# Rotated keys of the fifth layer: one full-width sum on VectorE and a head-table multiplication on GpSimd

## The reference, cut to what matters

```python
def _L2_xattn_ref(x, mem_seq, mem_mask, rms_scale, q_w, kv_w, out_w):
    ...
    q = jnp.einsum('BTD,NDH->BTNH', xn, q_w)
    kv = jnp.einsum('BSD,cKDH->cBSKH', mn, kv_w)
    k, v = (kv[0], kv[1])
    ...
    q = _apply_rope(q, q_pos) * HEAD_DIM ** (-0.5)
    k = _apply_rope(k, k_pos)
    q = q.reshape(B, T, NUM_KV, G, HEAD_DIM)
    logits = jnp.einsum('BTKGH,BSKH->BKGTS', q, k, preferred_element_type=jnp.float32)
    masked = jnp.where(mem_mask[:, None, None, None, :], logits, MASK_FILL)
    probs = jax.nn.softmax(masked, axis=-1).astype(x.dtype)
```

## Time and profile before

| | |
|---|---|
| median of 3 executions | 4558.1 us (4556.83 to 4559.51) |
| profiled execution, its own time | 4552.95 us |
| its span, first to last instruction | 4551.1 us |
| mean granted TensorE clock | 0.866 of 2.4 GHz |
| busy over the span | PE 87%, PEld 68%, DVE 66%, ACT 38%, POOL 17% |
| fifth layer | from 2901.1 us (the layer's first memset) to 3285.4 us (its last residual) |

### The profile page before, as it was taken

One profiled execution on the slowest core, in us unless ns is written; L12 is line 12 of the kernel. 1 busy time (PEld: TensorE's weight loads), 2 busy tenths in 40 slices (PEclk: granted clock), 3 DMA queues, 4 the chain that ended last, 5 costly groups with the idle time before them and its releaser, 6 DMA issues.

```text
span 4551.1 us, 105680 instructions
## 1 busy us (share of the span) xinstructions
PE 3947.3 (87%) x36890; PEld 3104.3 (68%) x36890; DVE 3006.2 (66%) x9082; ACT 1735.9 (38%) x4156; POOL 764.9 (17%) x575
## 2 busy tenths in 40 slices
PE   6999978888886888889999999777737899999965
PEld 4888855555554555589999999655537777777754
DVE  4666657777775777766666666799861355555569
ACT  3555534444442344333333333222203344444421
POOL 1222221111110000011111111100171122222211
PEclk9999987777776677689999999888758999999975
DMA  3000010000001000000000000100015200000000
GB/s 124 8 7 8 7 23 6 6 6 6 6 7 65 16 16 15 15 6 0 0 0 0 0 0 3 44 12 12 6 39 191 98 12 12 9 12 12 10 13 26
DMA packets 102053, 97.04 MB, mean 21 GB/s; under 512 B 31664, under 2 KB 91056, under 8 KB 101296
## 3 DMA queue, kind: packets, MB, share of 16 engines
q1 hardware_dynamic: 97408, 76.94, 5.6%
q0 software_dynamic: 4096, 8.40, 0.6%
q10 hardware_dynamic: 432, 10.19, 0.6%
HBM read 46.97 MB, written 19.66 MB: 15 GB/s over the span
## 4 chain that ended last, share of the span: by engine, by line
PE 60%; DVE 18%; SPq 8%; issue 7%; POOL 2%; DMA 2%; ACT 1%; DVEq 1%; POOLq 0%; ACTq 0%
PE ps L768 54%; SPq L591 7%; PE ps L936 5%; DVE acc L1658 2%; DMA arena_a<-kT 1%; DVE o_sb L1637 1%; POOL scr L718 1%; PE ps L806 1%; DVE arena_b L1606 1%; POOL route L740 1%; DVE xn L1442 1%; DVE x_sb L1557 1%; DVE st L1401 1%; DVE mx L1527 1%; DVE vsmall L1614 1%
## 5 line engine op out<-in xcount | busy, mean ns | idle before, releaser
L768 PE MATMUL ps<-xcT,small 128*128 128x256 f32 x2176 | 610.1, 419 | 34.7 <-DMA xcT<-in_ctxT 25.4
L732 POOL TENSOR_TENSOR rstd<-veps,neghalf 128x2 f32<-128x2 f32 (+1 forms) x224 | 167.9, 749 | 2403.8 <-DVE veps L1434 2071.2
L768 PEld LDWEIGHTS ps<-xcT,small 128*128 128x128 f32 x2176 | 411.3, 204 | 233.3 <-issue 114.5
L768 PE MATMUL ps<-arena_b,qT 64*64 64x64 f32 (+3 forms) x11136 | 541.8, 242 | 21.6 <-DVE arena_b L1606 20.3
L1278 ACT ACTIVATE kT<-ps 128x256 f32<-128x256 f32 (+1 forms) x768 | 294.4, 383 | 623.6 <-PE ps L768 547.4
L768 PE MATMUL ps<-small,xcT 128*64 128x64 f32 (+5 forms) x3072 | 482.7, 384 | 51.4 <-DVE acc L1658 30.3
L768 PE MATMUL ps<-xhi,parts_a 128*128 128x256 f32 (+1 forms) x2112 | 500.4, 289 | 22.7 <-DVE qT L1687 22.7
L768 PEld LDWEIGHTS ps<-arena_b,qT 64*64 64x64 f32 (+3 forms) x11136 | 463.5, 149 | 58.4 <-issue 35.0
L1248 ACT ACTIVATE pT<-ps 128x512 f32<-128x512 f32 (+1 forms) x576 | 303.3, 571 | 467.0 <-PE ps L936 465.3
L1687 DVE TENSOR_TENSOR qT<-kT,ps 128x256 f32<-128x256 f32 (+1 forms) x768 | 316.8, 419 | 188.5 <-ACT kT L1278 181.0
L768 PE MATMUL ps<-xlo,parts_a 128*128 128x256 f32 (+1 forms) x1536 | 430.6, 280 | 0.0
(11 more groups left out here) (212 smaller groups left out, 6388.5 us busy)
## 6 DMA issues: line engine op xcount, KB each, us to landing
wbuf<-parts_b SPq DMA_DIRECT2D x39, 512.0 KB, 3.0
arena_a<-kT SPq DMA_DIRECT2D x1024, 8.0 KB
xcT<-in_ctxT SPq DMA_DIRECT2D x96, 128.0 KB, 2.1
xn<-scr SPq DMA_DIRECT2D x39, 128.0 KB, 2.2
scr_y<-acc SPq DMA_DIRECT2D x39, 128.0 KB, 2.9
scr<-vsmall SPq DMA_DIRECT2D x9, 512.0 KB, 13.3
ctx_sb<-in_ctx SPq DMA_DIRECT2D x32, 128.0 KB, 2.1
arena_a<-in_w ACTq DMA_DIRECT2D x1, 4096.0 KB, 12.4
```

Source lines behind the costliest of these rows:

```text
L732: pool.tensor_tensor(rstd[:, 0:n], veps[:, 0:n], neghalf[:, 0:n], ALU.pow).then_inc(s_rstd.sem, 1)
L768: return nc.tensor.matmul(o, lhsT, rhs, start=start, stop=stop, skip_group_check=True)
```

## The change

DVE's four additions become one over 128 partitions and 256 columns, into the tile `kT` (unused in this layer until now). POOL then writes all four head blocks, zeros included, with one multiplication of 128 partitions x 1024 elements: the sum, read once for each head, times `own_rope`, a table of 128 x 4 that is 1 where the partition belongs to the head and 0 elsewhere. PE's `S0` now also waits for POOL (`s_krope`). POOL's memset of `k_rope` at the layer's start goes away. The table is made once, at the program's start, by a sum over blocks of 32 of the identity matrix on DVE.

```diff
@@ pool, start of L2X @@
+                    pool.wait_ge(s_krope0, 1)
                     for b in L1F.body_banks:
                         pool.wait_ge(drained[b], bank_base[4][b])
-                    pool.memset(arena_b[:, 0:2048], 0.0).then_inc(s_zero, 1)
                     pool.memset(vsmall[:, :, :], 0.0).then_inc(s_zero, 1)
@@ pool, do @@
+                if item == ("K", 0) and layer is L2X:
+
+                    u = layer.use(item)
+                    pool.wait_ge(drained[layer.front_ring.bank(g, u)], layer.front_ring.count(g, u))
+                    pool.tensor_tensor(k_rope(g.par).rearrange("p b (h k) -> p b h k", k=S),
+                                       k_sum(g.par).rearrange("p (b k) -> p b k", k=S).unsqueeze(2)
+                                       .to_broadcast([P, BPG, 4, S]),
+                                       own_rope[:, :].unsqueeze(1).unsqueeze(3).to_broadcast([P, BPG, 4, S]),
+                                       ALU.mult).then_inc(s_krope.sem, 1)
@@ pe, S0 @@
+                        if layer is L2X:
+                            pe.wait_ge(s_krope.sem, s_krope.after(g, 0))
@@ dve, start @@
-                    dve.wait_ge(s_zero, 4)
+                    dve.wait_ge(s_zero, 3)
...
+                    dve.tensor_reduce(own_rope[:, :], ident.rearrange("p (h d) -> p h d", d=32), AX_X,
+                                      ALU.add).then_inc(s_krope0, 1)
@@ dve, K of L2X @@
-                        for h in range(4):
-                            r0 = 32 * h
-                            last = dve.tensor_tensor(k_rope(g.par)[r0:r0 + 32, :, h * S:(h + 1) * S],
-                                                     c1[r0:r0 + 32], c2[r0:r0 + 32], ALU.add)
-                        last.then_inc(drained[b], 1)
+                        dve.wait_ge(s_krope.sem, s_krope.after(g.back(2), 0))
+                        dve.tensor_tensor(k_sum(g.par), qT[:, g.par, n + 2, :], qT[:, g.par, n + 3, :],
+                                          ALU.add).then_inc(drained[b], 1)
```

More of the change, by code:

```diff
@@ L289, in build @@
         onemu = sb("onemu", [P, 2])
+        own_rope = sb("own_rope", [P, 4])
         bv_col = sb("bv_col", [P, 1])
@@ L349, in build @@
         s_rope = step("s_rope", l2x=4)
+        s_krope = step("s_krope", l2x=1)
         s_mx = step("s_mx", **att)
@@ L383, in build @@
         s_bv = ctx.enter_context(nc.semaphore("s_bv"))
+        s_krope0 = ctx.enter_context(nc.semaphore("s_krope0"))
         s_ones = ctx.enter_context(nc.semaphore("s_ones"))
@@ L402, in build @@
         s_ready = ctx.enter_context(nc.semaphore("s_ready"))
-        steps = [s_stats, s_aggr, s_veps, s_rstd, s_xn, s_rope, s_mx, s_masked, s_sub,
+        steps = [s_krope, s_stats, s_aggr, s_veps, s_rstd, s_xn, s_rope, s_mx, s_masked, s_sub,
                  s_exp, s_sum, s_rv, s_probs, s_route, s_rexp, s_acc, s_act, s_mix, s_relu, s_upd, s_rank, s_xlo, s_res]
@@ L426, in k_rope, with k_sum @@
             return arena_b[:, par * 1024:(par + 1) * 1024].rearrange("p (b n) -> p b n", b=BPG)
+        def k_sum(par):
+            return kT[:, par, :]
         def v_small(par):
```

## The result

| | before | after |
|---|---|---|
| median of 5 executions | 4558.1 us (4555.49 to 4559.51) | 4581.23 us (4579.09 to 4584.71) |
| profiled execution, own time / span | 4552.95 / 4551.1 us | 4579.98 / 4577.4 us |
| mean granted TensorE clock | 0.866 | 0.863 |

The ratio is 1.0053, 95% interval 1.0038 to 1.0067: 23 us slower, 0.5%. Forecast were 4586 us, within 4571 to 4606.

A forecast was written before the change was run, and what follows sets the result against it. DVE, busy 94% of the layer's steady stretch, was taken to set the pace; +0.92 us a turn over 32 turns (29.4 us) less 1.5 at the starts gave +28 on 4558.1: 4586 us, range 4571 to 4606.

The forecast's parts named there:

- The sum: DVE's single remaining key addition of 128 x 256 from SBUF, in each turn: 0.42 us.
- DVE to POOL: Hand-over from DVE's last write of the key sum to POOL's start: 0.17 us.
- POOL's own time: POOL's multiplication of 128 x 1024 float32 in each turn: 1.90 us, with up to 2.2 allowed.
- The rival by which only the writes count: POOL's multiplication bound by its 1024 writes alone, 0.94 us, making the kernel faster: 4545 us; chance 4%.
- POOL made to wait for the running normalisation: POOL must let DVE's already started first normalisation finish before multiplying: 0.20 us.
- POOL to PE: Hand-over from POOL's multiplication to PE's start on the scores: 0.10 us.
- the half-clock seam: Stretch from key sum to softmax with scores at half clock, through PE: 4.21 us, against 3.17 before.
- The hold: DVE's normalisations from SBUF are held until POOL's multiplication ends; with POOL in second place, chance 57%.
- the case without one: Rival: normalisations not held and POOL not delayed, +0.59 us a turn, 4576 us; chance 19%.
- the full-clock seams: Stretches from key sum to softmax with scores at full clock, set by DVE's held work: 3.89 us.
- The wait added ahead of the sum: DVE's new wait, before the key sum, for POOL's work of two groups ago: costs nothing.
- The turn: One pipeline turn per group of 256 tokens in the fifth layer: from 11.7 to 12.6 us, +0.92.

The follow-up runs named there:

- first experiment: Changed kernel, but the fifth layer's four normalisations read unused PSUM banks instead of x and the context: 4582.09 us, ratio 1.0058.
- DVE's version of the multiplication: Changed kernel, but DVE adds the keys once and multiplies the four head blocks itself, POOL does nothing: 4562.99 us, ratio 1.0009.
- the run with M ahead of K: Changed kernel with the normalisations (M) ahead of the keys' sum (K) and the statistics ahead of the first softmax: 4596.7 us, ratio 1.0082.

## Why the prediction was right

The sign and the mechanism hold, and the time is near: 4581 against 4586 us. Part of that nearness is luck. The fifth layer was forecast to grow by 28 us and grew by 19.5; the fourth, in which nothing was forecast, grew by 3.9. By its steps:

- **The sum** 0.42, as measured. The table at the program's start costs 0.2 us, and DVE's work in the layer starts 1.7 us earlier, as forecast.
- **DVE to POOL** was taken as 0.17 and is 0.08 to 0.09. **POOL's own time** was taken as 1.90 from the other layers' multiplication: 1.89 with nothing beside it, so that spreading the second operand too costs nothing. The rival by which only the writes count falls.
- **POOL made to wait for the running normalisation**: taken as 0.20 from the earlier trace rows, it is 0.035 (1.927 against 1.892). That, 0.08 from the line above and 0.05 from **POOL to PE** (0.05 for 0.10) are the 0.3 us by which the half-clock seam was forecast too long: 4.21, measured 3.84 to 3.91.
- **The hold** is real, against the case without one, which had 19%. The Trainium skill (SBUF — State Buffer, section "SBUF: two separate sides") had it by its exclusive lock; the rows agree, with 2.17 us for two scalings that take 0.60, and 0.72 for those that read PSUM. But it decides only the full-clock seams, and those came out at 3.34 to 3.45 us where 3.89 was forecast: POOL ended sooner, and two normalisations rather than one were done at its end, with 0.95 us of DVE's work behind them instead of 1.2. In the half-clock turns, about two in three, the path through PE is the longer. POOL's end is common to both paths, so even where DVE's is the longer, dropping the hold gains nothing measurable (first experiment). The forecast gave 10 us to it.
- **The wait added ahead of the sum** was put at nothing, since its cover is a whole turn. It costs 0.09 us in every turn: from the start of the second product to the start of the keys' addition there were 0.45 us and are 0.54 in the mean. The order of instructions shows one more register instruction and one more wait there; which of the two takes the time, no run shows. DVE's version of the multiplication has the same 0.54. One turn of each (the additions start at 3111.59 and at 3103.47):

```profile
3111.14 0.41 DVE L1599 TENSOR_TENSOR qT<-ps,small 128x256 f32<-128x256 f32 x1
```
```profile
3102.94 0.41 DVE L1619 TENSOR_TENSOR qT<-ps,small 128x256 f32<-128x256 f32 x1
```

- **The turn** was to grow by 0.92 us and grew by 0.69 in the mean of 31. The 11.7 that the prediction gives for the turn of before is 0.1 too long: the steady ones take 11.59. In the 26 steady turns the growth is 0.62: the seam gives 0.53 of it (3.20 to 3.73 in their mean) and the addition's later start 0.09. The rest of DVE's turn, step by step, is the same to 0.01 us, so the granted clock of 0.78 instead of 0.81 costs nothing outside the seam. The first turn grew by 1.1 us and the last by 1.8; in the last, where DVE has no statistics to do, it now waits for PE at the second softmax and twice behind it. Thus most single terms of the seam were too high, one term outside it was put at nothing, and the sum of both came near.

Of the named signs, the lengthened POOL line (1.93), the stretched normalisation that ends with POOL and DVE's new wait for PE are there; that DVE's busy time would fall by 40 us was wrong, since held time counts as busy. Only with the hold removed does it: 288 us busy in 354 (first experiment's windows view of 2935.64 to 3290.01), where the changed kernel has 328 in 356 (2935.97 to 3291.71).

## What to carry to other kernels

Before work is taken off the busiest engine, look at the order in time for what waits on it: here the additions were themselves the first part of the path from the keys to the softmax, and only 1.43 us of normalisations and residuals behind them were its cover. Taking 1.27 us of additions off DVE and putting a slower engine in series (1.93 us for what DVE does in 1.22) made that path longer than the cover. In this kernel a shorter list on the bounding engine was worth something only where each place in which another engine's chain stood hidden was covered anew; moving the keys or the statistics alone opened the next such place each time. A long multiplication on GpSimd from SBUF ran beside DVE's work only where DVE's instructions there read PSUM or were statistics; scalings and two-operand additions from SBUF were held. And a whole-program time can carry a few us from a layer that the edit doesn't touch, so a small change is read in its own layer too.

## What the runs showed of the hardware

- POOL's multiplication holds a single-operand scaling of DVE from SBUF until it ends (2.17 us for two), and does not hold the same scaling from PSUM (0.72 for two).
- BATCH_NORM_STATS2 from SBUF is not held: in the run with M ahead of K, four of them keep their 0.49 and 0.47 us inside POOL's 1.89, while the small two-operand addition behind them is stretched from 0.17 to 0.36 and ends with POOL:

```profile
3108.39 1.89 POOL L747 TENSOR_TENSOR arena_b<-kT,own_rope 128x1024 f32<-128x1024 f32 x1 [8.66 <-DVE kT L1625]
```
```profile
3109.04 0.49 DVE L1421 BATCH_NORM_STATS2 st<-x_sb 128x6 f32 x2 [0.21 <-issue]
3109.44 0.47 DVE L1424 BATCH_NORM_STATS2 st<-ctx_sb 128x6 f32<-128x128 f32 x2
3109.94 0.36 DVE L1431 TENSOR_TENSOR agg<-st 128x4 f32<-128x4 f32 x1
```

- It works both ways, and POOL loses a little less than DVE's instruction has left when POOL starts. With 0.65 us left of a two-operand multiplication, POOL's 1.04 became 1.54 (all 32 turns); with 0.18 left of a single-operand scaling of 0.34, its 1.89 became 1.93. In both cases the loss is what was left less 0.14 to 0.15 us, an estimate from these two.
- POOL's short power of 128x4 elements does not hold a two-operand subtraction of DVE that starts 0.75 to 0.79 us into its 1.01: it keeps its 0.42 in all 30 such pairs, before and after the earlier trace rows.
- DVE needs 1.22 us for a product of 1024 columns with both operands spread by steps of zero, less than four additions of 256 columns (1.70); POOL needs 1.89.
